# Local attention in a four-layer block: both heads of a pair scored together and their weights turned together on TensorE

## The reference, cut to what matters

```python
bk, bv = look_around(bk), look_around(bv)      # each window sees itself and the one before it
sim = jnp.einsum('bhwid,bhwjd->bhwij', bq, bk)
sim = jnp.where(mask, -jnp.finfo(sim.dtype).max, sim)
attn = jax.nn.softmax(sim, axis=-1)
out = jnp.einsum('bhwij,bhwjd->bhwid', attn, bv)
...
x = x + o @ wo
```

## Time and profile before

| | |
|---|---|
| median of 3 runs | 2714.95 us (2709.14 to 2732.65) |
| the profiled execution | 2747.93 us, of which the span of the trace is 2746.1 us |
| TensorE matmul busy in the whole span | 2385.4 us (87%) |
| VectorE, ScalarE, GpSimd busy | 1256.0, 1060.3, 631.6 us |
| mean granted TensorE clock | 0.931 of full speed |

### The profile page before, as it was taken

One profiled execution on the slowest core, in us unless ns is written; L12 is line 12 of the kernel. 1 busy time (PEld: TensorE's weight loads), 2 busy tenths in 40 slices (PEclk: granted clock), 3 DMA queues, 4 the chain that ended last, 5 costly groups with the idle time before them and its releaser, 6 DMA issues. The chain is left out here.

```text
span 2746.1 us, 43410 instructions
## 1 busy us (share of the span) xinstructions
PE 2385.4 (87%) x13846; PEld 1737.5 (63%) x13847; DVE 1256.0 (46%) x2884; ACT 1060.3 (39%) x2525; POOL 631.6 (23%) x602
## 2 busy tenths in 40 slices
PE   7996496878998999899898998887999479988998
PEld 4664496634565864465685565456999446657887
DVE  4664101579666229866422664200000246637864
ACT  1663132223555224455421564113444116654332
POOL 1000201247221317521332000400000320035443
PEclk8997698989999999999998999988999789989999
DMA  7760442010000000000004660203221266400001
GB/s 180 156 139 3 144 168 72 16 38 0 24 0 21 15 16 0 23 0 0 12 1 85 123 122 34 86 23 108 108 81 53 63 124 133 85 26 18 24 24 37
DMA packets 115788, 163.94 MB, mean 60 GB/s; under 512 B 14459, under 2 KB 102254, under 8 KB 110670
## 3 DMA queue, kind: packets, MB, share of 16 engines
q1 hardware_dynamic: 109734, 148.68, 21.5%
q0 software_dynamic: 4608, 12.59, 1.4%
q10 hardware_dynamic: 1320, 1.03, 0.2%
HBM read 114.57 MB, written 47.32 MB: 59 GB/s over the span
## 5 line engine op out<-in xcount | busy, mean ns | idle before, releaser
L995 DVE TENSOR_REDUCE xa_mx<-ps 128x2 f32<-128x512 f32 x384 | 246.8, 686 | 107.7 <-PE ps L647 106.9
L141 PE MATMUL ps<-ones 128*128 128x384 f32 (+1 forms) x530 | 190.3, 484 | 98.9 <-DMA ex_tiles<-rows_out,rows_back 37.9
L854 ACT ACTIVATE xn_tok<-ps 128x512 f32<-128x512 f32 x384 | 210.5, 601 | 60.7 <-PE ps L655 57.3
L1513 PE MATMUL ps<-ex_tiles,ex_w 128*128 x1792 | 214.1, 279 | 7.3 <-issue 3.7
L1513 PEld LDWEIGHTS ps<-ex_tiles,ex_w 128*128 128x128 f32 x1792 | 213.5, 196 | 10.9 <-issue 8.1
L1519 PE MATMUL ps<-ex_w,ex_h 128*128 128x256 f32 x896 | 202.7, 379 | 0.0
L141 PEld LDWEIGHTS ps<-ones 128*128 128x128 f32 x530 | 107.6, 227 | 148.4 <-issue 59.5
L647 PE MATMUL ps<-xa_ks,xa_qs 48*128 48x256 f32 (+1 forms) x768 | 159.1, 325 | 33.5 <-DMA xa_qs<-x_maxima 12.0
L2139 PE MATMUL ps<-lo_w,lp_hs 128*128 128x512 f32 x384 | 176.5, 611 | 4.8 <-ACT lp_hs L2187 2.8
L1519 PEld LDWEIGHTS ps<-ex_w,ex_h 128*128 128x128 f32 x896 | 166.0, 190 | 20.2
L647 PEld LDWEIGHTS ps<-xa_ks,xa_qs 48*128 48x128 f32 (+1 forms) x768 | 108.6, 196 | 107.8 <-issue 55.8
(11 more groups left out here) (346 smaller groups left out, 5212.9 us busy)
## 6 DMA issues: line engine op xcount, KB each, us to landing
xa_ks<-x_keys SPq DMA_DIRECT2D x144, 128.0 KB
xa_qs<-x_queries SPq DMA_DIRECT2D x144, 128.0 KB, 4.6
ex_w<-in_L0f_w_dram SPq DMA_DIRECT2D x16, 1024.0 KB
ex_w<-in_L2f_w_dram SPq DMA_DIRECT2D x16, 1024.0 KB
x_keys<-xa_khl SPq DMA_DIRECT2D x24, 512.0 KB, 5.7
x_queries<-xa_qhl SPq DMA_DIRECT2D x24, 512.0 KB, 2.9
di_rows<-rows_in SPq DMA_DIRECT2D x16, 512.0 KB, 3.8
rows_out<-ex_tiles SPq DMA_DIRECT2D x62, 128.0 KB, 1.7
```

Of the source, the lines that this page charges most:

```text
L141: self.nc.tensor.matmul(self.ps[:, bank, 0:wide * P], self.ones[:], self.ones[:].unsqueeze(1).to_broadcast([P, wide, P]), start=True, stop ...
L854: nc.scalar.activation(pT[:, h % SLOTS].rearrange("p k q -> p (k q)"), c.ps[:, S_BANK + (HEADS * b + n) % 3], ACT.Exp).then_inc(exped.sem, 1)
L995: nc.vector.tensor_reduce(mx[:, half, :, col], c.ps[:, M_BANK + h % 2].rearrange("p (t n) -> p t n", t=2), AX_X, ALU.max).then_inc(max_put ...
L1513: ins = nc.tensor.matmul(c.ps[:, f % 4, 0:P], w1[:, par, k, f * P:(f + 1) * P], tile_of(n)[:, k], start=(k == 0), stop=(k == KD - 1))
```

## The change

Only TensorE's program is changed. `score` now takes a pair: it waits for the exponentials of the second of the two heads whose banks it will use, then issues both masks, both 128 x 128 scores (one head on the upper half of the array's rows, one on the lower), and both 128 x 256 scores. A `step` of a pair is: score pair hc + 2, weigh pair hc - 1, turn head 2hc, turn head 2hc + 1. The programs of ScalarE, VectorE and GpSimd are as before, and so are the number of instructions and the tiles.

```diff
-            def score(i, h):
-                r, hc = LD * (h % 2), h // 2
+            def score(i, hc):
                 pe.wait_ge(*q_staged(HC * i + hc + 1))
-                pe.wait_ge(*exped(LH * i + h + 1 - AHEAD))
-                bank = c.ps[:, 1 + h % AHEAD, :]
-
-                nc.tensor.matmul(bank[:, 0:3 * WIN], identb[:], maskb[:], start=True, stop=False)
-                nc.tensor.matmul(bank[:, 0:WIN], qst[r:r + LD, hc, 0:WIN], kst[r:r + LD, hc, 0:WIN],
-                                 start=False, stop=False)
-                nc.tensor.matmul(bank[:, WIN:3 * WIN], qst[r:r + LD, hc, WIN:S], kst[r:r + LD, hc, :],
-                                 start=False, stop=True).then_inc(scored.sem, 1)
+                pe.wait_ge(*exped(LH * i + 2 * hc + 2 - AHEAD))
+                banks = [c.ps[:, 1 + (2 * hc + j) % AHEAD, :] for j in range(2)]
+                for j in range(2):
+                    nc.tensor.matmul(banks[j][:, 0:3 * WIN], identb[:], maskb[:], start=True, stop=False)
+                for j, r in enumerate((0, LD)):
+                    nc.tensor.matmul(banks[j][:, 0:WIN], qst[r:r + LD, hc, 0:WIN], kst[r:r + LD, hc, 0:WIN],
+                                     start=False, stop=False)
+                for j, r in enumerate((0, LD)):
+                    nc.tensor.matmul(banks[j][:, WIN:3 * WIN], qst[r:r + LD, hc, WIN:S], kst[r:r + LD, hc, :],
+                                     start=False, stop=True).then_inc(scored.sem, 1)
...
-            def head(i, h, more=True, pair=None):
-                ahead(score, AHEAD, i, h, more)
-                if pair:
-                    weigh(*pair)
-                turn(i, h)
+            def step(i, hc, more=True, last=None):
+                if hc + 2 < HC:
+                    score(i, hc + 2)
+                elif more:
+                    score(i + 1, hc + 2 - HC)
+                if hc:
+                    weigh(i, hc - 1)
+                elif last is not None:
+                    weigh(last, HC - 1)
+                turn(i, 2 * hc)
+                turn(i, 2 * hc + 1)
 
             def sequence(i, more):
-                for h in range(2, LH):
-                    head(i, h, more, None if h % 2 else (i, h // 2 - 1))
+                for hc in range(1, HC):
+                    step(i, hc, more)
                 if more:
-                    head(i + 1, 0, True, (i, LH // 2 - 1))
-                    head(i + 1, 1)
+                    step(i + 1, 0, True, i)
                 else:
-                    weigh(i, LH // 2 - 1)
+                    weigh(i, HC - 1)
                 output(i)
 
-            for h in range(AHEAD):
-                score(0, h)
-            head(0, 0)
-            head(0, 1)
+            score(0, 0)
+            score(0, 1)
+            step(0, 0)
```

## The result

| | before | changed |
|---|---|---|
| median | 2713.9 us (4 runs) | 2822.8 us (4 runs, 2819.9 to 2833.7) |
| ratio | 1 | 1.0389, 95% interval 1.0356 to 1.0421 |
| profiled execution | 2747.9 us | 2821.1 us |
| granted clock, mean | 0.931 | 0.911 |

The changed kernel is slower by 109 us. The forecast was 2767 us, 52 us slower. The time lies inside the range of 2750 to 2850, but the loss is twice what the sum gave. Of all executions timed here one stood apart, at 4673 us (the kernel before with ScalarE's order changed); it is left out of the ratios.

A forecast was written before the change was run, and what follows sets the result against it. TensorE was taken as the bound, with ScalarE's chain only just covered. Stalled pairs, less the saving at the output, gave +3.45 us a sequence, +52 us in all: 2715 + 52 = 2767 us, range 2750 to 2850.

The forecast's parts named there:

- the sum: Stage total over both depths: +3.45 us a full sequence, 26.0 us a depth with the ends, +52 us in all.
- What bounds the kernel: In the stage, TensorE, busy 93%, is the bound; scores only just covered, waiting 0.21 us for ScalarE's exponentials.
- The score: TensorE's score of a pair: row halves work side by side, masks one after another; 1.39 us against 2.24, saving 0.85.
- The stall: Pair's score waits for ScalarE's puts and exponentials behind the last turn: 5.36 us a pair against 3.92, +1.44; 44 pairs stall.
- At and behind the output: Output covers the new wait, that pair 1.11 us shorter at 7.04; the next pair costs +1.68 us.
- the extra 0.24 us: Pair behind the output: VectorE normalises head 3 late, put 2.07 us after head 2's turn against 1.83.
- The clock: TensorE idles about 2.2 us in every 5.36, yet the clock was taken to stay full, adding nothing to the forecast.
- the signs of being wrong: In the changed stage: pairs below 3.9 us, scores of a pair over 2 us, or granted clock well under 1.00.
- The third rival: Clock falls to 1.2 GHz in stalled pairs and output: 203 us if throughout, half taken, about 2867 us; chance 0.18.
- One after another: Row halves do not overlap in the f32 scores: 2.24 us a pair, 92 us slower, 2807 us; chance 0.10.
- Little change: Some ScalarE work moves ahead of the turns, shortening the wait: within 27 us of before, about 2730 us; chance 0.06.
- Faster: Wait already satisfied when TensorE comes to it, pairs bound by TensorE at 2.95 us: -64 us, 2651 us; chance 0.04.

The follow-up runs named there:

- the runs on ScalarE's order: Changed kernel with ScalarE making exponentials of head h + 2 before the put of head h, 2719.4 us; with both puts, then two heads' exponentials, 2668.5 us.
- the three-filler run: Changed kernel with three matmuls of ones that add no result ahead of each stalled score: 2765.9 us, 1.0186 of before.
- the fillers: Matmuls of ones over 384 columns into an unread PSUM bank, added to the changed kernel's stalls: one 2767.0 us, two 2766.3, three 2765.9.
- the wait-alone run: Kernel before, head-by-head order kept, but a score waits for the exponentials of both heads of the pair whose banks are taken over: 2916.7 us, 1.0723.
- the one-filler run: Changed kernel with one matmul of ones, adding no result, in each stall in place of three: 2767.0 us, 1.0181 of before.
- the run with the exponentials first: Changed kernel with ScalarE's two calls of a head swapped, exponentials of head h + 2, then put of head h: 2719.4 us, 0.9997 of before.

## Why the prediction was right in its direction and half too small

**What bounds the kernel.** Right. The busy share called TensorE the bound, the small wait of 0.21 us in the earlier trace rows showed how little slack ScalarE's chain had. The wait alone, put into the old order, costs 60 to 69 us at a full clock.

**The score.** Right: 1.29 us for a pair against 1.39. The term that was too large is the second mask. Two masks take 0.43 us (747.89 to 748.32), not 0.54, since a mask that is followed by another costs 0.50 - 0.34 = 0.16. The likely reading is that the 0.27 of the earlier trace rows holds the change from the whole array to row halves, which now comes once; no run parts it from the change from bf16 to f32 at the same place. The two matmuls of L2326, at the other end, took 0.52 us, and the four of L2327 take 0.53 (748.65 to 749.18). The Trainium skill ("TensorEngine Tiling (Array Packing)", Key Properties) has such a change of mode drain the engine, and it would have set the pair 0.09 lower; the trace agrees in size, 0.10 us, though it was saved on the way in. Masks in a row and halves side by side are together worth 40 to 44 us at the full clock, by the runs with the scores one after another.

**The stall.** Right, in place and cause, and near in size: 5.28 us a pair (5.36), a gap of 2.32 us at the full clock (2.2), 50 us in all (52). The runs on ScalarE's order show the cause: with one exchange in it the gap is 1.13 us, with another it is gone, and the time follows.

**At and behind the output.** The stall is covered at the output, as said: from the turn of head 0 to that of head 2 it is 7.13 us (749.98 to 757.11) against 7.04. Behind it the extra 0.24 us was too much: that pair takes 5.36 us, 0.08 more than the others, not 5.60, since the second put starts 1.92 us after the turn of head 2 (757.11 to 759.03) and not 2.07. A sequence is 23.05 us against 23.38. That the 23.43 of the three-filler run lies so near the forecast is luck: the third filler adds 0.38.

**The clock.** Here the prediction failed. The step that failed is the choice to put the clock's term at nothing. It said: "I take the first, because scores, weighings and the output are long runs of matmuls." showed both outcomes, and the choice between them rested on that one likeness, a gap of 2.65 us ahead of a long run. In the changed kernel the clock in the stage was 0.79, and the fillers show that this is 57 us (58 by the stages), more than the stall itself. It was one of the signs of being wrong that the prediction named. That the time still fell into the range, which reached to 2850 for such a case, does not make the sum right. The third rival, with 0.18, was the case that came; its price was also too high, 100 us for half of the time. Two sizes in it were off. The clock was not at the lower level for half of the time: 0.79 is 42% of it. And the terms on the chain don't double: the lower level adds 1.05 us to the score, 0.67 to the weighing and 0.37 to the way from turn to put (744.34 to 745.36 is 1.02 against 0.65), 2.09 us in place of 2.84, and 7.36 - 5.28 = 2.08 for the whole pair.

**The other rivals.** One after another, 2807: the run that makes it so gives 2810 at a full clock. Little change, 2730: no part of ScalarE's work moved ahead of the turns by itself; where an edit moves one head's exponentials ahead of its put, the time is 2719. Faster, 2651: with ScalarE's order changed this is where the kernel goes, 2668 and then 2643. Its condition, that the wait is satisfied when TensorE comes to it, was named rightly and was not met by the change.

**What stays open.** Which pattern loses the clock. From 700 to 850 us the wait-alone run had the shortest gaps of the slow ones (1.39 us) and the lowest clock (0.66), though TensorE was shown as busy for 84% of the stretch; the changed kernel, with gaps of 2.01 to 2.32 us, had 0.75 and 74%, the one-filler run, with gaps of up to 1.67 us, 0.93 and 78%. Neither the gap nor the busy share puts these in order. The runs show that fillers bring the clock back and what that is worth, not what the chip counts.

## What to carry to other kernels

When work of one engine is merged into larger steps, follow each wait of the new step back to what the same engine issued just before it: if another engine stands between and its order is unchanged, the step waits for a round trip, and the saving never shows. Change the orders of the engines together; here the same pairs cost 109 us alone, and the kernel gained 78 us with them and two small changes of order elsewhere. And price a new gap on TensorE twice, once as idle time and once as the clock that it may take from the work around it; a filler in the gap tells the two apart in one run.

## What the runs showed of the hardware that was not expected

- An f32 score of two heads on the two row halves took 1.29 us where one head takes 1.12.
- The lower clock level did not double the times: 2.34 against 1.29 us for a score of a pair, 1.47 against 0.80 for a weighing, 1.02 against 0.65 us from a turn to the copy that reads it.
- Gaps of 1.39 us, once in a pair, brought the granted clock from 1.00 to 0.66 in the wait-alone run and cost 135 us; gaps of 1.13 us left it at 0.96 in the run with the exponentials first, and gaps of 1.67 us with one filler in each at 0.93.
- One added matmul in each gap, 0.81 us of busy time at the full clock and computing nothing, made the changed kernel 56 us faster (2767.0 against 2822.8 us).
